# Where the last unit of a two-layer cross-attention kernel sums its probabilities: products with ones on TensorE in place of additions on GpSimd

## The reference

```
q = einsum('bte,ef->btf', emb, Wq) + bq
k = einsum('bml,le->bme', latent, Wk) + bk
v = einsum('bml,le->bme', latent, Wv) + bv
w = softmax(einsum('bte,bme->btm', q, k) * scale, axis=1)
x = einsum('btm,bme->bte', w, v) + emb
out = (x - mean(x)) * rsqrt(var(x) + EPS) * gamma + beta
```

## Time and profile before

| | us |
|---|---|
| median of 3 runs | 1006.89 (1006.8 to 1008.17) |
| profiled execution, own time | 1007.27 |
| its span, first to last instruction | 1005.5 |
| PE busy in the span | 988.2 |
| DVE, ACT, POOL busy | 869.5, 670.6, 562.5 |
| mean granted TensorE clock | 0.998 of full |

### The profile page before, as it was taken

One profiled execution on the slowest core, in us unless ns is written; L12 is line 12 of the kernel. 1 busy time (PEld: TensorE's weight loads), 2 busy tenths in 40 slices (PEclk: granted clock), 3 DMA queues, 4 the chain that ended last, 5 costly groups with the idle time before them and its releaser, 6 DMA issues. The chain is left out here.

```text
span 1005.5 us, 23866 instructions
## 1 busy us (share of the span) xinstructions
PE 988.2 (98%) x6940; PEld 929.7 (92%) x6940; DVE 869.5 (86%) x2605; ACT 670.6 (67%) x1882; POOL 562.5 (56%) x521
## 2 busy tenths in 40 slices
PE   7999999999999999999999999999999999999996
PEld 6889999999999999999999999999999999999996
DVE  4889888988988898888988988898888898888877
ACT  3466766666766776776766676776676666676664
POOL 0134566555657555657555656655656655565754
PEclk9999999999999999999999999999999999999999
DMA  8644444454443454443454443454444445444211
GB/s 217 165 83 87 103 97 81 102 116 96 96 99 77 98 116 98 98 100 75 96 113 98 98 102 85 89 107 99 103 100 93 79 104 115 100 96 99 44 35 52
DMA packets 373959, 98.33 MB, mean 98 GB/s; under 512 B 308488, under 2 KB 357786, under 8 KB 373914
## 3 DMA queue, kind: packets, MB, share of 16 engines
q1 hardware_dynamic: 371370, 96.98, 43.9%
q10 hardware_dynamic: 2544, 0.80, 0.4%
HBM read 83.06 MB, written 14.68 MB: 97 GB/s over the span
## 5 line engine op out<-in xcount | busy, mean ns | idle before, releaser
L722 PE MATMUL oq_bank<-probs,raw 125*128 125x224 f32 x1464 | 297.8, 353 | 0.4 <-ACT probs L1009 0.4
L722 PEld LDWEIGHTS oq_bank<-probs,raw 125*128 125x128 f32 x1464 | 267.8, 190 | 0.6 <-issue 0.6
L987 ACT ACTIVATE probs<-probs,neg_max 125x224 f32<-125x224 f32 x378 | 177.8, 472 | 133.4 <-DVE neg_max L1375 133.2
L1751 POOL TENSOR_TENSOR psum<-probs 125x672 f32<-125x672 f32 x61 | 98.6, 1616 | 240.6 <-ACT probs L1009 240.6
L698 PE MATMUL score_bank<-qT_hi,cT_hi 128*125 128x224 f32 x768 | 199.2, 286 | 1.1 <-ACT qT_hi L979 0.6
L699 PE MATMUL score_bank<-qT_hi,cT_lo 128*125 128x224 f32 x768 | 188.6, 272 | 0.0
L1009 ACT ACTIVATE probs<-probs,rsum 125x224 f32<-125x224 f32 x378 | 150.9, 471 | 11.5 <-DVE rsum L1395 10.0
L1831 POOL TENSOR_TENSOR y_out<-z,gamma_row 112x512 f32<-112x512 f32 x60 | 90.3, 1528 | 109.9 <-ACT z L1033 109.9
L698 PEld LDWEIGHTS score_bank<-qT_hi,cT_hi 128*125 128x125 f32 x768 | 144.7, 188 | 5.7 <-issue 3.6
L703 PE MATMUL score_bank<-qT_lo,cT_hi 128*125 128x224 f32 x768 | 147.1, 272 | 0.7 <-DVE qT_lo L1358 0.7
L1375 DVE CUSTOM_DVE_ANT_0 probs<-score_bank,d_row 125x224 f32<-125x224 f32 x384 | 138.6, 380 | 8.5 <-PE score_bank L703 4.5
(11 more groups left out here) (151 smaller groups left out, 2105.6 us busy)
## 6 DMA issues: line engine op xcount, KB each, us to landing
raw<-in_ctx_dram SPq DMA_DIRECT2D x64, 375.0 KB
cb<-in_ctx_dram SPq DMA_DIRECT2D x248, 92.0 KB
x<-in_x_dram SPq DMA_DIRECT2D x32, 448.0 KB, 3.6
xb<-in_x_dram SPq DMA_DIRECT2D x124, 112.0 KB, 2.7
out_dram<-y_out SPq DMA_DIRECT2D x31, 448.0 KB, 6.3
cb<-in_ctx_dram SPq DMA_DIRECT2D x124, 3.5 KB
y<-in_L_xattn_Wq_dram SPq DMA_DIRECT2D x2, 512.0 KB, 5.3
Wq_next<-in_L_xattn_Wq_dram SPq DMA_DIRECT2D x2, 512.0 KB, 12.9
```

The source lines that it names most:

```text
L722: ins = nc.tensor.matmul(o, raw[0:MP, u.slot, c, cols], probs[0:MP, u.par4, c, :], start=(c == 0), stop=(c == MC - 1))
L987: ins = act.activation(probs[0:MP, u.par4, c, :], probs[0:MP, u.par4, c, :], ACT.Exp, bias=neg_max[0:MP, u.par4, c:c + 1], scale=-1.0, acc ...
L1751: pool.tensor_tensor(psum3[0:MP, :, :], probs[0:MP, u.par4, 0:HALF, :], probs[0:MP, u.par4, HALF:MC, :], ALU.add).then_inc(psum3_done, 1)
```

## The change

GpSimd's five additions in the last unit are gone. Instead TensorE takes each chunk of the probabilities, directly behind that chunk's two o products, as the weights of two products with ones (one for each half h), accumulated over the six chunks. The two halves now accumulate in two banks, `t_bank[1]` and `t_bank[0]`, and since `t_bank[0]` held the d row before, TensorE waits for `d_done` ahead of chunk 0. The wait for `psum_done` is gone. Two orders are changed too. On DVE, `o_lo` of the last unit moves ahead of `front_scale(v, 1)`, and at the end `last_scale(u, 0)` moves ahead of `last_centre(u, 1)`. On ACT, the mean of half 1 moves from ahead of its squares to the very end.

```diff
             def last_o_product(u):
 
+                pe.wait_ge(d_done, u.n())
                 for c in range(MC):
                     wait_last_probs(pe, c)
                     for l in range(LC):
@@
                         if c == MC - 1:
                             ins.then_inc(o_ready, 1)
-
-                pe.wait_ge(psum_done, u.n())
+                    last_r_part(u, c)
+
+            def last_r_part(u, c):
+
                 for h in range(TH):
-                    ins = nc.tensor.matmul(last_r[:, h:h + 1], psum_all[0:MP, h * TP:(h + 1) * TP], ones[0:MP, 0:1],
-                                           start=True, stop=True)
-                ins.then_inc(last_r_ready, 1)
+                    ins = nc.tensor.matmul(last_r[h], probs[0:MP, u.par4, c, h * TP:(h + 1) * TP], ones[0:MP, 0:1],
+                                           start=(c == 0), stop=(c == MC - 1))
+                if c == MC - 1:
+                    ins.then_inc(last_r_ready, 1)
...
-            for h in range(TH):
-                mean_of(u, slice(h, h + 1), last_mean_done)
-                sum_squares(u, h, last_square_done)
-                variance_of(u, slice(h, h + 1), last_square_done)
+            mean_of(u, slice(0, 1), last_mean_done)
+            sum_squares(u, 0, last_square_done)
+            variance_of(u, slice(0, 1), last_square_done)
+            sum_squares(u, 1, last_square_done)
+            variance_of(u, slice(1, 2), last_square_done)
+            mean_of(u, slice(1, 2), last_mean_done)
...
             front_centre(v, 1)
-            front_scale(v, 1)
             o_lo(u, 0, True)
             o_lo(u, 1, True)
+            front_scale(v, 1)
             residual(u, 0, True)
             add_and_sum(u, 0)
             residual(u, 1, True)
             add_and_sum(u, 1)
             last_centre(u, 0)
+            last_scale(u, 0)
             last_centre(u, 1)
-            last_scale(u, 0)
             last_scale(u, 1)
...
             inverse_deviation(v)
-            last_sum_probs(u)
             for h in range(TH):
                 last_inverse_deviation(u, h)
```

More of the change, by code:

```diff
@@ L259, in build_xattn @@
         last_probs_done = sem("last_probs_done")
-        last_psum_done = sem("last_psum_done")
         last_r_ready = sem("last_r_ready")
@@ L331, in build_xattn @@
         front_r = t_bank[1][0:TP, 0:TH]
-        last_r = t_bank[1][0:TP, TH:2 * TH]
+        last_r = [t_bank[1][0:TP, TH:TH + 1], t_bank[0][0:TP, 0:1]]
         def wait_last_probs(eng, c):
@@ L1427, in residual @@
                     dve.wait_ge(ln_done, u.n(-UNIT_GAP, 2))
-                dve.scalar_tensor_tensor(out=y[0:TP, u.par, h, :], in0=bv_row[0:TP, u.layer, :], scalar=(last_r if at_end else front_r if is_in_front(u) else r_psum)[:, h:h + 1],
+                dve.scalar_tensor_tensor(out=y[0:TP, u.par, h, :], in0=bv_row[0:TP, u.layer, :], scalar=last_r[h] if at_end else (front_r if is_in_front(u) else r_psum)[:, h:h + 1],
                                          in1=(x0, x1)[u.layer][0:TP, u.slot, h, :],
@@ L1784, in front_sum @@
                     pool.tensor_tensor(psum3[0:MP, 0, :], of, probs[0:MP, u.par4, c, :], ALU.add).then_inc(front_psum_done, 1)
[L1786 to L1802, removed]
             def last_inverse_deviation(u, h):
```

## The result

| | before | changed |
|---|---|---|
| median of 22 runs each, us | 1007.04 (1006.35 to 1008.17) | 1008.28 (1007.66 to 1009.41) |
| ratio of the two, 95% interval | | 1.0013 (1.0007 to 1.0019) |
| profiled execution: own time, span | 1007.27, 1005.5 | 1008.14, 1006.3 |
| granted clock over the span | 0.998 | 0.999 |

The medians are 1.24 us apart: the change makes the kernel 0.13% slower, which is within the 0.2% named as no change but clear of its own noise, since the interval leaves out 1. The forecast was +1.0 and 1007.9 us. With 22 runs in place of three the median of before is 1007.04 and not 1006.89, which is 0.15 of the 0.38 between forecast and measured time.

A forecast was written before the change was run, and what follows sets the result against it. TensorE, busy 988 of 1005.5 us, was taken to bound the body, so only the tail could move: +1.11 for the first sum, -0.1 at the end, +1.0 on 1006.89 gives 1007.9 us, 8-in-10 range 1006.5 to 1009.3.

The forecast's parts named there:

- TensorE sets the pace of the last o products: Last unit: o records 0.193 us apart with one 0.2 us hold, so work added between chunks pushes the end.
- The price of a pair: Two products with ones behind a chunk's o products: 0.32 us each, five ahead of chunk 5, net 1.52.
- The bound named: A pair without cover on its left takes 0.42 us, as in the profile before.
- What starts when: After the last o product: 0.19 and the sixth pair's 0.32 later, value products start at 996.28, 0.62 later than before.
- the displaced scale: `front_scale(v, 1)` on DVE, now behind `o_lo` with nothing to hide it: 0.5 of the first sum's 1.11 us delay.
- The tail: From the second sum to the last scale: 3.14 us before, gain 0.06 to 0.11, taken as 0.1.
- The sum: Whole kernel: +1.11 for the later first sum, -0.1 for the end, together +1.0 us.
- Rival A: Products with ones nearly hidden on TensorE: the end comes 0.5 us earlier, 1006.4; chance 0.13.
- Rival B: GpSimd's half-1 `rstd` locked out until centre 1 ends: +1.3, or +1.8 with pairs at 0.42; chance 0.14 with Rival D.
- Rival C: One-column products drop TensorE's clock to 1.2 GHz from 996.3, doubling value products: +3.8 us, 1010.7; chance 0.05.
- Rival D: GpSimd's wait never held TensorE: the end comes 1.5 to 1.8 us later; chance 0.14 with Rival B.

The follow-up runs named there:

- e2: Changed kernel with the products with ones of chunks 0 to 4 removed, only chunk 5's pair left; ratio to the kernel before 0.9994.
- e3: Changed kernel with the products with ones of chunks 0 to 4 issued twice; ratio to the kernel before 1.0033.
- e1: Changed kernel with `front_scale(v, 1)` put back ahead of the two low parts of o; ratio to the kernel before 1.0006.
- e5: Kernel before with only the tail's new order on VectorE and ScalarE; traced once, last scale at 12.02 us from the first o product, before 12.16.
- e6: Changed kernel with GpSimd adding chunks 0 to 4, TensorE multiplying only chunk 5 and that sum with ones; ratio to the kernel before 0.9994.
- e4: Changed kernel with all pairs behind the last o product and `front_scale(v, 1)` ahead of the low parts; traced once, last scale at 14.42 us.
- e9: The kernel of e4 again, timed; ratio to the kernel before 1.0025, last scale at 12.98 us in its trace.
- e10: Changed kernel with pairs of chunks 3 to 5 behind the last o product and `front_scale(v, 1)` ahead of the low parts; ratio to before 1.0009.
- e11: The kernel of e6 again, to narrow its interval; ratio to the kernel before 0.9999, last scale at 11.58 us.

## Why the prediction was right, point by point

- **TensorE sets the pace of the last o products.** Right. The reading that decided the sign was the distance of the records, 0.19, with a single hold; e2 and e3 give a straight line, the last o record begins at 4.36, 6.39 and 8.35 us with none, five and ten pairs ahead of it.
- **The price of a pair.** Too small: 0.32 taken, 0.40 measured. The error is in the step "the next product begins 0.32 after". It does, but the o records behind it start later: the second of them 0.27 after the first instead of 0.19. In the trace the weight load of that second record starts 0.08 after the first record, where in the steady stream it starts with it. The bound named, 0.42 without cover, was nearer. The same delay of 0.08 stood in the trace before at chunk 2, where a load was held; the prediction rightly booked it as saved (e2: 4.36 against 4.44), but did not see that each pair makes it anew. 5 x 0.40 - 0.08 = 1.92 against 1.95 measured for the o products, where 1.52 was forecast. This is the term of the sum that was sized too small. The estimate from the Trainium skill (page "TensorE: Matmul & The Clock Gate", section "LDWEIGHTS (loading the stationary operand)"), four loads at 93 ns, gives 0.37 and stands nearer to the 0.39 to 0.41 of e2 and e3 than the row that I preferred to it. The prediction's remark that the row's 0.32 agrees if the first load hides is loose. By the same figure of that page three loads would be an estimate of 0.28.
- **What starts when.** The value products begin 0.51 after the last o record in the changed kernel, as forecast (0.19 + 0.32).
- **VectorE.** Right: the displaced scale has nothing to hide it. 0.48 by e1, 0.5 forecast. From the first value product to the first sum, 2.13 against the forecast's 2.14.
- **The tail.** Gains 0.14 to 0.15 (e5 and the changed kernel: 2.99 and 2.99 in place of 3.14); 0.1 was taken. What the sum had too high was the time from a centre to its scale, 0.85 and not 0.90.
- **The sum.** +1.95 - 0.90 for TensorE (its idle time and the uncovered pair gone), +0.48 for the scale, -0.15 for the tail, 1.38 against 1.37 measured. The forecast had +1.52 - 0.90 + 0.5 - 0.1 = 1.0: it had the five pairs 0.43 too small, and it took 0.02 too much for the scale and 0.05 too little for the tail's gain, which leaves the difference of 0.36.
- **Rival A** (hidden pairs) falls by e2 and e3. **Rival B** falls: `rstd` of half 1 ends 0.41 after scale 0, while centre 1 still runs, so GpSimd gets in between two VectorE instructions. `rstd` took 0.68, shorter than the 1.06 of before, because it started later inside scale 0: both end 0.41 after it. The sentence of the Trainium skill (page "SBUF — State Buffer", section "Who interferes with whom") that the holder keeps the shared port for its whole instruction agrees with that end. A second VectorE instruction with two inputs in SBUF, queued directly behind, did not keep the port from GpSimd in the changed kernel and in e1, e5 and e6. **Rival C** did not happen in the changed kernel (1.00 from 994 to 1000), but a fall of the clock behind one-column products is real, by e4 and e9. **Rival D** falls: without GpSimd's sum the value products start 0.51 after the last o record, where they started 1.41 after it before.

## What to carry to other kernels

Work moved from a waiting engine's neighbour onto the engine itself is only free as far as it fits into the wait: here there were 0.8 us of idle time in one place, and the change put five sixths of its 2.4 us ahead of that place, where the engine was full. Split such work by time, as e6 does: leave to the other engine what it finishes early, and give to the waiting one only the last piece. And price a one-column product by what a row of them measures (here 0.10 a record, 0.20 an fp32 product) and by what its successor loses, not by its one column.

## What the hardware showed that was not expected

- A row of 24 one-column fp32 records (2.4 us), in which TensorE's weight loads are busy throughout, was followed by the 1.2 GHz level in one of two profiled executions (e4: 0.71 and 0.50 in the two windows behind it), at a price of 1.4 us at the last scale (14.42 against 12.98). Six of the ten timed runs of the same kernel have a lower clock over the span too (0.996 or 0.997, against 0.998 and 0.999 in the changed kernel and the other experiments). The kernel before, which idles 0.8 us there, and e10 with 12 such records kept 1.00.
- A pair of one-column products delays the stream twice: the next o record begins 0.33 us after the pair's first record, and is itself followed by the second after 0.27 us instead of 0.19, each time. Together that is 0.40, no more than the 0.39 of a pair behind another pair (e3).
- An fp32 product stands in the trace as two records; those of 224 columns are 0.19 us apart, where the score products' records of the same 224 columns are 0.11 apart. The "two passes" of the description ahead of the prediction count records and not their time.
- Executions of the same body reach the same instruction up to 2 us apart (989.3 to 991.3 over the kernels here). For a change at the end of a kernel the distance from a near landmark repeats to 0.05 us (e6 and e11: 11.59 and 11.58; e4 and e9 until the clock differs: 6.83 and 6.83), where the medians of ten runs resolve about 1 us.
